# A graph attention layer on one core: other group sizes, a denser sort, a reordered drain and another layer norm at the end

## The reference

```python
q = (x[src] @ qW).reshape(e, 4, 24)
k = (x[dst] @ kW).reshape(e, 4, 24)
v = (x[dst] @ vW).reshape(e, 4, 24)
exp_s = exp(clip(einsum('ehd,ehd->eh', q, k), -10, 10))
norms = segment_sum(exp_s, src, 6250)[src]
w = exp_s / (norms + 1e-8)
res = segment_sum(w[:, :, None] * v, src, 6250).reshape(6250, 96)
out = layernorm(x + x + res, eps=1e-5)       # mean and variance over the 96 features
```

## Time and profile before

| | |
|---|---|
| median of 3 runs | 1357.38 us |
| profiled execution | 1364.9 us |
| its span, first to last instruction | 1363.1 us |
| mean granted TensorE clock | 0.709 of 2.4 GHz |
| busy: PE, DVE, ACT, POOL | 77%, 75%, 49%, 70% |
| first gather, last gather start | 121.4 us, 1310.1 us |
| chain that ended last, by engine | POOL 39%, DVE 18%, issue 16%, PE 14%, ACT 7% |

### The profile page before, as it was taken

How to read it: one execution, slowest core, us unless ns; L and a number is a source line. 1 busy time by engine, 2 the same in 40 slices (tenths; PEclk the granted TensorE clock), 3 DMA queues, 4 the chain that set the end, 5 groups by cost and what they waited for, 6 DMA issues and landing times.

```text
span 1363.1 us, 23400 instructions
## 1 busy us (share of the span) xinstructions
PE 1050.7 (77%) x6502; PEld 935.0 (69%) x6503; DVE 1019.2 (75%) x2846; ACT 674.0 (49%) x1464; POOL 957.1 (70%) x911
## 2 busy tenths in 40 slices
PE   6896498776798786798887778887678888888850
PEld 4674497665787665698776667777577777777740
DVE  8797998689997678998758887777655555555556
ACT  4773299522599522399842225886232222222215
POOL 1203777777787777777777777777777777777745
PEclk9897599956699856599877555889665555555555
DMA  4300222222222222222222222222422222222212
GB/s 121 121 0 25 68 70 70 73 79 70 68 67 69 76 70 73 70 72 72 70 74 79 77 72 74 70 72 82 135 79 78 78 78 78 78 79 78 77 41 71
DMA packets 68298, 100.62 MB, mean 74 GB/s; under 512 B 33522, under 2 KB 53874, under 8 KB 68204
## 3 DMA queue, kind: packets, MB, share of 16 engines
q0 software_dynamic: 42240, 86.56, 23.3%
q1 hardware_dynamic: 25964, 12.94, 3.3%
HBM read 92.23 MB, written 7.22 MB: 73 GB/s over the span
## 4 chain that ended last, share of the span: by engine, by line
POOL 39%; DVE 18%; issue 16%; PE 14%; ACT 7%; DMA 4%; DVEq 2%; POOLq 0%; ACTq 0%; SPq 0%
POOL kv L466 39%; ACT steps_m L672 4%; PE ps_r L620 3%; DMA kv<-kv_table,dst_s 2%; DVE acc L1031 2%; PE ps_q L608 2%; DVE steps_m L800 2%; DVE prod L1039 2%; PE ps_a L594 1%; DVEq L392 1%; PE ps_b L594 1%; DMA acc<-in_x_dram 1%; DVE place_m L940 1%; DVE place_m L944 1%; ACT onehT L717 1%
## 5 line engine op out<-in xcount | busy, mean ns | idle before, releaser
L466 POOL DMA_INDIRECT kv<-kv_table,dst_s x880 | 921.9, 1048 | 329.5 <-issue 322.8
L620 PE MATMUL ps_r<-wv,oneh 128*128 128x100 f32 x1760 | 344.9, 366 | 127.4 <-DVE wv L1046 126.3
L620 PEld LDWEIGHTS ps_r<-wv,oneh 128*128 128x128 f32 x1760 | 312.5, 270 | 150.2 <-DVE wv L1046 141.1
L608 PE MATMUL ps_q<-qt,onehT 128*128 x1760 | 327.3, 353 | 90.9 <-ACT onehT L717 85.9
L608 PEld LDWEIGHTS ps_q<-qt,onehT 128*128 128x128 f32 x1760 | 298.3, 259 | 119.7 <-issue 118.6
L672 ACT ACTIVATE steps_m<-iota_f,pos_t 125x283 f16<-125x283 f32 (+4 forms) x778 | 321.3, 502 | 22.1 <-PE ps_b L594 13.9
L1031 DVE TENSOR_TENSOR acc<-acc,ps_r 128x100 f32 x880 | 223.2, 254 | 65.6 <-issue 32.4
L1039 DVE TENSOR_TENSOR prod<-ps_q,kv 128x480 f32<-128x480 f32 x176 | 115.3, 655 | 208.9 <-DMA kv<-kv_table,dst_s 201.2
L710 ACT ACTIVATE wv<-clipped 128x20 f32<-128x20 f32 x176 | 38.2, 217 | 433.1 <-DVE clipped L1073 432.9
L594 PE MATMUL ps_a<-steps_m,place_m 125*128 125x283 f16 (+4 forms) x778 | 197.8, 294 | 1.7 <-ACT steps_m L672 0.2
L717 ACT ACTIVATE onehT<-ps_t 128x640 f32<-128x640 bf16 x176 | 123.4, 701 | 148.6 <-PE ps_t L629 143.9
(11 more groups left out here) (185 smaller groups left out, 696.4 us busy)
## 6 DMA issues: line engine op xcount, KB each, us to landing
kv<-kv_table,dst_s POOLq DMA_INDIRECT x880
kv_table<-kv SPq DMA_DIRECT2D x7, 672.0 KB, 3.6
acc<-in_x_dram SPq DMA_DIRECT2D x6, 336.0 KB, 4.6
steps_m<-in_x_dram SPq DMA_DIRECT2D x6, 336.0 KB, 5.3
out_dram<-kv SPq DMA_DIRECT2D x6, 336.0 KB
src_i<-in_src_dram SPq DMA_DIRECT2D x1, 415.0 KB
dst_i<-in_dst_dram SPq DMA_DIRECT2D x1, 415.0 KB
acc<-in_x_dram SPq DMA_DIRECT2D x1, 288.0 KB, 5.7
```

The lines of the kernel that those rows point to most:

```text
L466: nc.gpsimd.indirect_dma_start(kv[:, nm, u, :], None, kv_dram, bass.IndirectOffsetOnAxis(ap=dst_s[:, n * U + u:n * U + u + 1], axis=0)).th ...
L608: last = nc.tensor.matmul(ps_q[nm % 2][:, u * D:(u + 1) * D], onehT[:, nm % 2, u * P:(u + 1) * P], qt[:, bass.ds(blks[u], 1), :].rearrange ...
L620: last = nc.tensor.matmul(ps_r[nm % 2][:, u * RW:(u + 1) * RW], oneh[:, nm % 2, u, :], wv[:, nm % 2, u, :], start=True, stop=True)
```

## The change

The kernel after differs in five places.

1. `GC` goes from 180, 150, 170, 190, 160 to 140, 110, 140, 190, 270 columns. The groups then give 17, 22, 27, 37 and 73 iterations of tiles (before 25, 29, 33, 38 and 51), and theta is 186, 205, 234, 283 and 361 wide (before 225, 244, 264, 283, 254).
2. The plan. A group's rank pieces and its units are spread evenly over the iterations that there are; an iteration now holds one or two units (`sorts` is a list). The iteration for PE's last unit is gone, and `differ` and `turn` stand behind the same iteration. `LS` is (3, 4, 4, 4).
3. Prologue. The projections are called elsewhere in the ranking of group 0; x has four buffers; only group 0's columns of `src` are loaded first; three wide constants are made by ACT and eight tiny ones by POOL, not by DVE.
4. Drain. In the last iterations DVE has another order (`weigh` first, then the additions), and the last iteration's five products go to five PSUM banks with a semaphore each, so that an addition can start behind its own matmul.
5. End. One `bn_stats` for each row block replaces the reduction for the mean, the subtraction, the square and the second reduction. The reciprocal of the first chunk comes ahead of the rest. POOL's multiplications wait for DVE's addition of the chunk before (`s_two`). ACT scales with scale and bias, four parts; DVE scales the last 10 of the 49 rows blocks.

```diff
-    GC = [180, 150, 170, 190, 160]
+    GC = [140, 110, 140, 190, 270]
+    LS = (3, 4, 4, 4)
-        project_after = {"mark0": (0,), "count": (1,), "base0": (2, 3), "sel0": (4,), "table": (5, 6)}
+        project_after = {"mark3": ("lift",), f"tally{len(ROUNDS[0]) - 1}": (0,), "count": (1,), "base1": (2,),
+                         "table": (3, 4, 5, 6)}
+        for g in range(1, G):
+            end = B0[g] - LS[g - 1]
+            count = end - m - 2
+            names = rank(g) + ["choose"]
+            units = V0[g + 1] - V0[g] + 1
+            ranked = round(count * (12 * GC[g] + 1000) / (34 * GC[g] + 1000))
+            at = shares(len(names), ranked)
+            for k in range(ranked):
+                m = plan_iters(m, 1)
+                for name in names[at[k]:at[k + 1]]:
+                    PLAN.append(("piece", name, g))
+            at = shares(units, count - ranked)
+            PLAN.append(("iters", m, g, [tuple(range(V0[g] + a, V0[g] + b)) for a, b in zip(at, at[1:])]))
+            m = plan_iters(m + count - ranked, 1)
+            PLAN.append(("piece", "differ", g))
+            PLAN.append(("piece", "turn", g))
+            m = plan_iters(m, 1)
+            PLAN.append(("piece", "pick", g))
...
 # ACT, tiles()
                 if sorts:
-                    unit(*sorts, halves=(1,))
+                    unit(*sorts[0], halves=(1,))
+                for sort in sorts[1:]:
+                    unit(*sort)
...
 # POOL, end
+            for i in range(NPC):
+                pool.wait_ge(s_den, 1 if i == 0 else 2)
+                wait(pool, s_two, i)
+                nc.gpsimd.tensor_tensor(y, y, den...to_broadcast([P, PC, HEADS, DH]), ALU.mult).then_inc(s_div, 1)
...
 # ACT, end
+            for j, (a, b) in enumerate(PARTS):          # (0, 1), (1, 3), (3, 5), (5, 7)
+                act.wait_ge(s_var, j + 1)
+                nc.scalar.activation(std[...], var[...], ACT.Sqrt).then_inc(s_std, 1)
+                act.wait_ge(s_inv, j + 1)
+                for i in range(a, min(b, NPC - 1)):
+                    for k in range(PC if i < NPC - 2 else HALF):
+                        last = nc.scalar.activation(yout[i][:, k, :], acc[:, n, 0:D], ACT.Identity,
+                                                    scale=inv[:, n:n + 1], bias=shift[:, n:n + 1])
...
 # DVE, end
+                for n in range(i * PC, (i + 1) * PC):
+                    last = nc.vector.bn_stats(stats[:, n, :], acc[:, n, 0:D])
+            for j, (a, b) in enumerate(PARTS):
+                for i in range(a, b):
+                    total(i)
+                    if j and i == a:
+                        scale_of(j - 1)
+                spread_of(j)
+            scale_of(len(PARTS) - 1)
```

More of the change, by code:

```diff
@@ L67, in gnn, with plan_iters, plan_last, shares @@
     PLAN = []
[L69 to L89, removed]
+    def plan_iters(m, count, units=()):
+        units = list(units) + [()] * (count - len(units))
+        PLAN.append(("iters", m, 0, units))
+        return m + count
+    def plan_last(m):
+        looped = max(m, R)
+        PLAN.append(("iters", m, 0, [()] * (looped - m)))
+        reps = max(0, NBT - L - looped) // R
+        PLAN.append(("loop", looped, reps))
+        PLAN.append(("iters", looped + reps * R, 0, [()] * (NBT + 2 - looped - reps * R)))
+    def shares(count, parts):
+        return [count * k // parts for k in range(parts + 1)]
     def plan():
@@ L107, in plan @@
         m = -L
[L108 to L115, removed]
-                m = plan_iters(m, 1)
[L117 to L124, removed]
+        for g in range(1, G):
[6 more added lines that the diff above has]
+            for k in range(ranked):
+                m = plan_iters(m, 1)
+                for name in names[at[k]:at[k + 1]]:
[7 more added lines that the diff above has]
+            PLAN.append(("piece", "pick", g))
             assert m == end
-        plan_iters(m, NBT + 2 - m)
+        plan_last(m)
     plan()
@@ L966, in unit @@
             def unit(g, v, vm, between=lambda i: None):
+                if isinstance(v, int) and v == 0:
+                    dve.wait_ge(s_wide, 1)
                 wait(dve, s_bin, v - 1)
@@ new lines, in tiles @@
+                blks = None
+                if isinstance(m, int) and m >= NBT - 1:
+                    if m == NBT - 1:
+                        coming[m - 1] = blocks_of(mybir.EngineType.DVE, m - 1)
+                        coming[m] = blocks_of(mybir.EngineType.DVE, m)
+                    blks = coming[m - 2]
+                    weigh()
+                    if m - 2 < NBT - 1:
+                        dve.wait_ge(s_res, m - 2 + 1)
+                    for u in range(U):
+                        add_up(u)
+                    multiply()
+                    reduce()
+                    clip()
+                    return
@@ L1051, in tiles @@
+                if isinstance(m, int) and m == NBT - 2:
+                    coming[m - 1] = blocks_of(mybir.EngineType.DVE, m - 1)
+                multiply()
+                weigh()
                 if there(m - 2):
```

315 lines of the change are left out of this document (165 added, 150 removed).

## The result

The changed kernel takes 1393.55 us (median of 4 runs, 1391.63 to 1394.99); the kernel before took 1357.62 beside it (4 runs). The ratio is 1.0254, with a 95% interval of 1.0227 to 1.028: slower by 36 us. The forecast was 1351 us, with a range of 1319 to 1374. The profiled execution took 1393.8 us, its span 1392.0, at a mean granted clock of 0.703.

The account below looks back on a forecast made before the run. POOL's gathers were taken to bound the kernel before, and the compute engines the changed one ahead of its last group. Terms: -28.6 + 37 - 4 - 10.5 = -6, giving 1351 us as a median; range 1319 to 1374.

Parts of the forecast that it names:

- The bound: In the gathers: POOL bounds the kernel before; after the change compute needs 768 us before the last group, POOL 735.
- Rival A: From first gather to last: compute hides under POOL's gathers, costing +5 instead of +37; 1319 us, chance 0.22.
- The prologue, -28.6: Before the gathers: first gather near 92.8 us instead of 121.4, saving 28.6; bounds -20 to -34.
- Rival C: Before the gathers: loads hold pay or the projections, sort starts at 54 as before; 1359 us, C and rest 0.12.
- The middle, +37: First gather to last: last group comes 33 us late, gathers end after 1228 us, costing 37; bounds +5 to +70.
- the sum of 768 us: First gather to last group's dst_s: ranking, sort stages and last-theta-to-dst_s of four groups, 122 + 155.5 + 202 + 288.5 us.
- the handoff: From a group's last theta to dst_s: 16.5 us, and 19.5 for 365 tiles, with 1.39 of waiting before differ.
- Where POOL stops: POOL idle ahead of gathers for dst_s: 2 us before the second group, 20 and more before the fifth, 30 to 50 in all.
- Rival B, TensorE: In the last sort stage: PE decides below a mean clock of 0.84; at 0.7, 193 us and 1383 total; chance 0.16.
- The drain, -4: From the last prod to the last addition: 5.7 us instead of 9.7, saving 4.
- the end, -10.5: Layer norm and stores after the last addition: 30 us against 40.6, saving 10.5; bounds -3 to -13.
- The rule on the shared pair: In sort stages: if tensor_tensor leaves descriptor writes alone, units cost gathers nothing, POOL's 735 us becomes some 680, sum unchanged.

Follow-up runs that it names:

- the sizes halfway: The changed kernel with groups of 160, 130, 150, 190, 220 columns, all else as changed: 1345.71 us, ratio 0.9896 to the kernel before.
- ACT's copies moved: The changed kernel with ACT's copies of the sorted sums (cum_a, cum_b) ahead of its work of the iteration following the last unit: 1370.68 us.
- two units first: The changed kernel with each sort stage's two-unit iterations first and one-unit iterations last, same number of iterations: 1389.46 us.
- shared thetas: The changed kernel with two of each unit's ten thetas in groups 1 to 4 made by DVE instead of ACT: 1364.95 us.

## Why the prediction was wrong

*The bound.* Right, and it decided the case: the compute engines' own sum stands ahead of the last group, and POOL behind it. The sizes of before, the sizes halfway and the changed ones have it under, near and far over POOL's time, with 0, 14 and 78 us of gaps. Rival A, that the compute hides, is refuted by them.

*The prologue, -28.6.* There were two errors. The first gather came at 97.6, not 92.8: counting began at 20.55 us, where the forecast had 17, because `pay` waited 4.3 us for the load of `dst`. That was named as the bound of -20, and not taken.

```profile
14.59 0.23 DVE L810 TENSOR_SCALAR src_i<-src_i 125x140 int32<-125x140 int32 x1 [4.30 <-DMA dst_i<-in_dst_dram]
20.55 0.87 DVE L838 TENSOR_REDUCE cnt_f<-kst_m 125x49 f32<-125x686 f16 x1
49.30 0.35 PE L595 MATMUL ps_a<-onehT,place_m 125*128 125x186 f16 x1 [2.63 <-ACT steps_m L682]
```

PE began the sort at 49.3 (46 forecast), and the units went at the 2.85 us that were taken for them. The second error: the 121.4 it was measured against is found in that one execution alone; against 116.9 the gain is 19.3 us, and with the old sizes nothing is left of it, so it comes from 40 columns less: 0.48 us a column. Rival C had the mechanism (a load holds `pay`) at too large a size: the sort was to start at 54, and theta began at 47.

*The middle, +37.* It measured +64 against the profiled kernel before (1253.4 us of gathers and gaps, from 1189.7), and as much against the kernel's second profile. That is inside the bounds of +5 to +70, but not for the reason of the upper one, which was TensorE. The step that failed is the sum of 768 us for the compute engines alone, 24 short, in two of its terms. The first is ACT in the sort stages, taken as an engine without a gap, 383 us: its own work is right to 3 us, but ACT stands still 4 to 6 us in each stage (mostly for the clip and the transposes at its start), 19 in all. The second is the handoff, priced at 16.5 to 19.5 us by the waits of one handoff in which a single unit went ahead: behind a packed stage the four took 80 us, not 70. Ranking came 6 cheaper. The mechanism stands: with ACT's copies moved the four stretches sum to 769 us, 24 less than in the changed kernel, and the time falls by 23; nothing hides an error in this sum.

*Where POOL stops.* 30 to 50 us of idle time for `dst_s`, growing from 2 to 20, was forecast; it is 33.8, in nearly equal pieces of 8, 6, 10 and 10. The rest of the loss is in waits for buffers, because compute was already three iterations behind. The sum doesn't depend on it.

*Rival B, TensorE.* Refuted as stated: the last sort stage had a clock of 0.92, well over the 0.84 named, and PE was busy 144 of 166.8 us. A lower clock does cost time at the handoffs, where no one looked for it.

*The drain, -4, and the end, -10.5.* Together they are 11.0 less than before (41.0 us behind the last gather within the span, from 52.0), not 14.5. That is 3.5 of the 4.8 in the table; the other 1.3 are the prediction's own sum, for 768 + 460 against the 1189.7 of before is +38.3, and it wrote +37. In the drain the last prod now stands behind the scatter and the additions of the iteration ahead: it starts 3.3 us after the last gather, before it was 1.7; from it to the last addition are 6.3 us, forecast 5.7. In the end seven `bn_stats` take 1.22 us, as was taken for them. The last root waits for ACT's scaling, and the last reciprocal stands still 2.30 us for it (1.5 were allowed):

```profile
1354.28 0.65 DVE L1059 TENSOR_TENSOR prod<-ps_q,kv 128x480 f32<-128x480 f32 x1
1359.90 0.66 DVE L1041 TENSOR_TENSOR acc<-acc,ps_t 128x100 f32 x2
1363.61 1.22 DVE L1151 BATCH_NORM_STATS2 stats<-acc 128x6 f32<-128x96 f32 x7
1368.07 2.61 ACT L751 ACTIVATE kv<-acc,shift,inv 128x96 f32<-128x96 f32 x7 [0.78 <-DVE shift L1171]
1379.24 5.12 ACT L751 ACTIVATE kv<-acc,shift,inv 128x96 f32<-128x96 f32 x14 [0.52 <-DVE shift L1171]
1384.50 0.24 DVE L1170 RECIPROCAL inv<-std 128x14 f32<-128x14 f32 x1 [2.30 <-ACT std L746]
```

Fourteen scalings take 5.12 us. The forecast's row gave 3.9, with one operand of [128,1]. The Trainium skill (ScalarE: Activation LUTs, What ACT_TABLE_LOAD costs) adds some 93 ns for each such operand, which gave the estimate of 5.2; the trace agrees with it, 2.61/7 = 0.37 us against 0.28 in the earlier trace rows.

*The rule on the shared pair.* The prediction weighed what the Trainium skill (SBUF — State Buffer, Who interferes with whom) infers, that tensor_tensor leaves the writing of descriptors alone. Gathers average 110.15/102 = 1.08 us in the last sort stage and 0.95 in plain iterations behind it. The rows show where the longer ones lie, under the three tensor_tensor of a unit:

```profile
859.39 0.95 POOL L475 DMA_INDIRECT kv<-kv_table,dst_s  x1 [0.30 <-issue]
861.90 0.82 DVE L986 TENSOR_TENSOR place_m<-place_m,pay_a 125x1280 f16<-125x1280 f16 x1
861.96 1.58 POOL L475 DMA_INDIRECT kv<-kv_table,dst_s  x1 [0.30 <-issue]
862.81 0.82 DVE L988 TENSOR_TENSOR place_m<-place_m,pay_b 125x1280 f16<-125x1280 f16 x1
863.85 0.95 POOL L475 DMA_INDIRECT kv<-kv_table,dst_s  x1 [0.30 <-issue]
```

Over the whole trace, of the gathers with a unit's products near them, the 125 that overlap these for over 0.3 us take 1.31 us on average, the 137 that overlap none 0.98; in the kernel before it is 1.33 and 0.96. This case doesn't bear the inference out, though no run takes these instructions away alone. The forecast's sum didn't depend on it.

*The sign.* No single term had the wrong sign. The forecast was a small difference, -6, of large terms, and all four stretches were off to the same side: 4.8, 24.1, 1.3 and 4.8, and 7.5 more came from the execution it was measured from. The range of 1338 to 1363 gave the middle ±9; the sum of 768 us came out 3% short, and that alone is 24.

## What to carry over

When a pipeline of groups lies under a long row of gathers, compare for each group the compute needed before it with the time of the gathers ahead of it. Behind the first group, whose columns the prologue pays at 0.48 us each, sizes cost little as long as every group stays under; past that point each us is paid in full, so a last group much larger than its neighbours is dear, and one more group of moderate size was cheap. Price a handoff by the whole chain through all in-order queues (PE's own work ahead of it, ACT's copies behind it), not by the wait seen in one instance, and look at the granted clock in it as well. And profile the kernel before a second time before a gain is taken from its prologue.

## What the hardware showed

- Seven `bn_stats` of 128x96 take 1.22 us, 0.17 each in a row, while one alone spans 0.24.
- A second operand of [128,1] on ACT costs 0.09 us an instruction (0.28 to 0.37 for 96 elements).
- In the handoff of the last group PE stands still for 3.03 us at 2.4 GHz, and 1.1 us behind that gap its clock falls to 1.2 GHz:

```profile
865.70:878.00 12.30, 7.25 (x55) 6.12 (x53) 4.07 (x12) 4.83 (x11) 6.90 (x8) 1.00 0.64 158
878.00:884.30 6.30, 6.30 (x34) 5.57 (x34) 2.50 (x9) 0.98 (x3) 1.95 (x3) 0.52 1.01 231
```

The ten matmuls of the products take 2.45 us there, and 1.25 one iteration ahead. In the kernel with ACT's copies first this stretch stays at 1.00. At all twelve handoffs of the changed kernel and of those with two units first and with shared thetas PE has such a gap, of 2.6 to 3.0 us, and the clock falls within 2 us of its end. But a gap of this length doesn't always bring a fall. In the changed kernel's last sort stage PE stands still from 805.0 to 808.0, and the clock is 1.00 until 827; in the kernel with the copies first it stands still just ahead of the handoff, and the clock is 1.00 until 864.8:

```profile
849.66 0.34 PE L596 MATMUL ps_a<-steps_m,place_m 125*128 125x361 f16 x1 [3.09 <-ACT steps_m L683]
```

What decides between the two is open, and so is whether the gap in the handoff is the cause of the fall there: no run tried it by itself.
